# Moving sums, centring and small factors of the last stages from VectorE to GpSimd in a two-layer attention and expert kernel

## The reference

```python
x = x + attention(layernorm(x), ctx, mask)        # layer 0: softmax over the unmasked rows of ctx
x = x + experts(layernorm(x), Wr, Wg, Wu, Wd)     # 8 experts, the 2 best of each row, SiLU
x = x + topk_attention(layernorm(x), W_q, W_o, ctx)  # keeps the 54 largest of 1601 scores of each row
x = x + bitffn(layernorm(x), w1, w2)

def bitlinear(x, w):                              # used twice, with gelu between
    xs = 127.0 / clip(max(abs(x), axis=-1), 1e-5);  xq = clip(round(x * xs), -128, 127) / xs
    ws = 1.0 / clip(mean(abs(w)), 1e-5);            wq = clip(round(w * ws), -1, 1) / ws
    return einsum('bsd,hd->bsh', xq, wq)
```

## Time and profile before

| what | value |
|---|---|
| time, median of 3 runs (lowest, highest) | 443.55 us (442.79, 444.75) |
| profiled execution: its time, its span | 437.4 us, 435.7 us |
| busy of the span: PE, DVE, ACT, POOL | 81%, 69%, 42%, 11% |
| chain that ended last, by engine | PE 43%, DVE 31%, issue 13%, DMA 7% |

### The profile page before, as it was taken

One profiled execution on the slowest core, in us unless ns is written; L12 is line 12 of the kernel. 1 busy time (PEld: TensorE's weight loads), 2 busy tenths in 40 slices (PEclk: granted clock), 3 DMA queues, 4 the chain that ended last, 5 costly groups with the idle time before them and its releaser, 6 DMA issues.

```text
span 435.7 us, 6602 instructions
## 1 busy us (share of the span) xinstructions
PE 353.8 (81%) x2075; PEld 282.1 (65%) x2082; DVE 299.9 (69%) x760; ACT 181.5 (42%) x312; POOL 49.4 (11%) x100
## 2 busy tenths in 40 slices
PE   0899999999899996089898989878968872656984
PEld 0466777777799895047578988766655561625863
DVE  2432445762311024537999999999999999999983
ACT  2062353442534233024337255437656610443485
POOL 4100000115000001760000000170100000000010
PEclk9999999999999999559999999989998995969899
DMA  7583886609478992845878996453450031413301
GB/s 251 178 260 116 296 301 215 185 25 346 146 230 265 308 292 90 251 160 188 249 229 265 294 326 202 153 157 121 118 185 14 0 118 46 116 35 105 114 15 48
DMA packets 70809, 76.38 MB, mean 175 GB/s; under 512 B 5356, under 2 KB 69496, under 8 KB 70776
## 3 DMA queue, kind: packets, MB, share of 16 engines
q1 hardware_dynamic: 57272, 59.93, 44.0%
q10 hardware_dynamic: 11968, 11.84, 8.3%
q0 software_dynamic: 1536, 4.20, 2.9%
HBM read 66.91 MB, written 9.04 MB: 174 GB/s over the span
## 4 chain that ended last, share of the span: by engine, by line
PE 43%; DVE 31%; issue 13%; DMA 7%; ACT 2%; POOL 1%; SPq 1%; ACTq 0%; DVEq 0%; POOLq 0%
PE S L868 13%; PE GU L946 9%; DVE fold L1233 6%; DVE cand_h L1221 6%; PE A L895 6%; DVE cand_l L1228 5%; PE O L956 4%; DVE fold L1238 3%; PE A L899 3%; PE T L882 3%; DMA xg<-xs 2%; DMA v_sb<-ctx 2%; DVE row L1261 2%; DMA x_res<-x 2%; DVE gabs L1327 2%
## 5 line engine op out<-in xcount | busy, mean ns | idle before, releaser
L637 ACT ACTIVATE pT<-T 128x512 f32<-128x512 f32 x64 | 31.4, 514 | 79.0 <-PE T L882 74.9
L899 PE MATMUL A<-pT,v_sb 128*128 128x128 f32 (+1 forms) x416 | 54.1, 287 | 8.1 <-ACT pT L637 4.7
L946 PE MATMUL GU<-xgT,wg_ring 128*128 128x128 f32 x480 | 58.6, 276 | 2.1 <-DVE hid L1160 1.1
L946 PEld LDWEIGHTS GU<-xgT,wg_ring 128*128 128x128 f32 x480 | 56.9, 192 | 4.3 <-issue 1.9
L899 PEld LDWEIGHTS A<-pT,v_sb 128*128 128x128 f32 (+1 forms) x416 | 51.6, 202 | 10.9 <-issue 6.6
L1221 DVE MAX8 cand_h<-fold 128x8 f32<-128x801 f32 x56 | 55.0, 991 | 0.0
L868 PE MATMUL S<-k_sb,qT 128*128 128x400 f32 (+2 forms) x128 | 47.6, 518 | 4.4 <-ACT qT L694 1.3
L895 PE MATMUL A<-v_sb,pT 128*128 128x256 f32 (+1 forms) x208 | 49.6, 381 | 0.9 <-DMA v_sb<-ctx 0.9
L868 PE MATMUL S<-k_sb,xT 128*128 128x400 f32 (+2 forms) x128 | 48.5, 515 | 0.8 <-ACT xT L622 0.8
L1233 DVE MATCH_REPLACE8 fold<-cand_h,fold 128x801 f32<-128x801 f32 x48 | 47.1, 984 | 0.0
L895 PEld LDWEIGHTS A<-v_sb,pT 128*128 128x128 f32 (+1 forms) x208 | 37.9, 190 | 7.7 <-DMA v_sb<-ctx 1.5
(11 more groups left out here) (153 smaller groups left out, 488.4 us busy)
## 6 DMA issues: line engine op xcount, KB each, us to landing
v_sb<-ctx SPq DMA_DIRECT2D x36, 512.0 KB, 4.2
wg_ring<-Wg SPq DMA_DIRECT2D x30, 256.0 KB
wg_ring<-Wu SPq DMA_DIRECT2D x30, 256.0 KB
wd_ring<-Wd SPq DMA_DIRECT2D x30, 256.0 KB
k_sb<-ctxT SPq DMA_DIRECT2D x16, 400.0 KB, 5.4
xg<-xs ACTq DMA_DIRECT2D x30, 128.0 KB, 3.8
ys<-y_sb ACTq DMA_DIRECT2D x30, 128.0 KB, 3.5
k_sb<-ctxT SPq DMA_DIRECT2D x8, 402.0 KB, 4.2
```

The costliest lines, as they stand in the source:

```text
L637: act.activation(pT[0:r, i % NPT, :, :].rearrange("p a s -> p (a s)")[:, 0:w], t_bank("pT", *key)[0:r, 0:w], ACT.Copy).then_inc(pTe_done, 1)
L899: mm = pe.matmul(A_bank[:, o * P:(o + 1) * P], v[0:r, a, o * P:(o + 1) * P], pT[0:r, j, a, :], start=m == 0 and o == 0, stop=m == NMC - 1 ...
L946: mm = pe.matmul(gu_bank(*key)[:, a * F + f * P:a * F + (f + 1) * P], wg_ring[:, w % NWG, a, k, f * P:(f + 1) * P], cols[:, k, :], start=k ...
```

## The change

Seven steps move to other engines, for some or all tiles. For tiles 0 to 5 the sum `x3` becomes two steps: `x3a` (ACT takes the product out of PSUM, scaled, into `xn4`) and `x3p` (POOL adds it to `x_res`). `fin` becomes `fina` and `finp` in the same way; tiles 6 and 7 keep `x3` and `fin` on DVE. For all eight tiles `cent`, `va4`, `xmx`, `xscl`, `xdeq` and `gdeq` move from DVE to POOL. `cut`, the masking, stays on DVE. `WIDE_FROM` goes from 9 to 6, so the values of tiles 6 and 7 go round through five homes, three of which held layer 0's values. `ORDER` is written anew throughout; the second weight's `wqb` comes later in it.

```diff
+SUM_POOL = (0, 1, 2, 3, 4, 5)
-WIDE_FROM = 9
+WIDE_FROM = 6
...
 # gpsimd block
+                elif op == "x3p":
+                    t = key[0]
+                    pool.wait_ge(x3a_done, n("x3a", t))
+                    pool.wait_ge(norm_done, n("norm", 3, ROW_OF[t]))
+                    pool.tensor_tensor(x_res[:, t, :], xn4[:, t % 2, :], x_res[:, t, :], ALU.add).then_inc(x3p_done, 1)
+                elif op == "finp":
+                    t = key[0]
+                    pool.wait_ge(fina_done, n("fina", t))
+                    pool.tensor_tensor(fin[:, t % 2, :], fin[:, t % 2, :], x_res[:, t, :], ALU.add).then_inc(finp_done, 1)
...
+                elif op == "va4":
+                    pool.tensor_scalar(var4[:, t:t + 1], mv4[:, t, 1:2], EPS, None, ALU.add).then_inc(va4_done, 1)
...
+                elif op == "cent":
+                    pool.tensor_scalar(xn4[:, t % 2, :], x_res[:, t, :], mv4[:, t, 0:1], None, ALU.subtract) \
+                       .then_inc(cent_done, 1)
...
 # scalar block
+                elif op == "x3a":
+                    act.wait_ge(wo_done, n("wo", t))
+                    act.wait_ge(rc3_done, n("rc3", t))
+                    if t >= 2:
+                        act.wait_ge(q4_done, n("q4", t - 2))
+                    act.activation(xn4[:, t % 2, :], O_bank[:, 0:D], ACT.Copy, scale=r3[:, t:t + 1]).then_inc(x3a_done, 1)
+                elif op == "fina":
+                    act.wait_ge(dn_done, n("dn", t))
+                    act.wait_ge(gdeq_done, n("gdeq", t))
+                    act.activation(fin[:, t % 2, :], O_bank[:, 0:D], ACT.Copy, scale=gdeq[:, t:t + 1]).then_inc(fina_done, 1)
...
 # vector block: va4, cent, xmx, xscl, xdeq, gdeq are gone; st4 waits for x3p_done for tiles 0 to 5
-                elif op == "xscl":
-                    dve.scalar_tensor_tensor(out=xscl[:, t:t + 1], in0=xinv[:, t:t + 1], scalar=127.0,
-                                             in1=rstd4[:, t:t + 1], op0=ALU.mult, op1=ALU.mult).then_inc(xscl_done, 1)
...
 # ORDER, its end
-ginv.7 fin.5 gmul.7 gdeq.7 dn.6 store.5 h4T.7 fin.6
-h4e.7 store.6 dn.7 fin.7 store.7
+ginv.7 fin.6 gdeq.7 gmul.7 store.6 h4T.7 h4e.7 dn.7 fin.7 store.7
```

More of the change, by code:

```diff
@@ L137 @@
-merge.3 va4.1 thr.3 wo.2 upd.6.1 rs4.1 exp3.3 gabs.0.0 s3.4.1 xmx.1 stats.3.3 x3.2 gabs.0.1 st4.2 s3e.4.0 aggr.3.3
-gmx.0 s3e.4.1 ag4.2 s3.4.2 xinv.1 ginv.0 var.3.3 xdeq.1 gmul.0 gdeq.0 rstd.3.3 cut.3.0 s3.4.3 s3e.4.2 xscl.1 va4.2
-cent.2 xmul.1 rs4.2 s3.5.0 norm.3.3 s3e.4.3 xabs.2 xmx.2 pairH.4 s3.5.1 ldk.3.3.0 s3e.5.0 pairL.4 pT.3.3.0 maxH.4.0
-ldk.3.3.1 s3e.5.1 s3.5.2 pTe.3.3.0 maxL.4.0 h4T.0 repH.4.0 ldk.3.3.2 s3e.5.2 s3.5.3 h4e.0 xdeq.2 maxH.4.1 q4.1
-pvm.3.3.0 repL.4.0 ldk.3.3.3 s3e.5.3 q4e.1 repH.4.1 up.1.0 maxL.4.1 ldv.3.3.2 up.1.1 gelu.1.0 dn.0 xinv.2 maxH.4.2
@@ new lines @@
+cut.7.0 up.5.0 gelu.5.1 cut.7.1 pT.3.7.0 gelu.5.0 cut.7.2 pT.3.7.1 pTe.3.7.0 cut.7.3 rc3.7 pTe.3.7.1 pvm.3.7.0
+gabs.5.0 rc3.6 x3.6 st4.6 ag4.6 gabs.5.1 pT.3.7.2 cent.6 pvm.3.7.1 gmx.5 va4.6 pTe.3.7.2 xabs.6 rs4.6 ginv.5 gabs.4.1
+gmul.5 xmx.6 xdeq.6 xinv.6 gabs.4.0 xscl.6 pT.3.7.3 pvm.3.7.2 gdeq.5 xmul.6 gmx.4 pTe.3.7.3 ginv.4 gdeq.4 gmul.4 q4.6
+pvm.3.7.3 q4e.6 h4T.4 aTe.7 up.6.1 h4e.4 wo.7 gelu.6.1 up.6.0 x3.7 h4T.5 gelu.6.0 st4.7 dn.4 ag4.7 gabs.6.1 h4e.5
+cent.7 gabs.6.0 va4.7 fina.4 rs4.7 gmx.6 dn.5 ginv.6 xabs.7 gdeq.6 gmul.6 xmx.7 xdeq.7 xinv.7 xscl.7 finp.4 xmul.7
```

260 lines of the change are left out of this document (131 added, 129 removed).

## The result

The changed kernel took 449.68 us (median of 4 runs, 448.32 to 454.17), the kernel before in the same session 443.17 (4 runs, 442.35 to 444.75): slower by 6.5 us where 4.5 less were forecast, and outside the range of 433.5 to 445.0. Either way the changed kernel is slower; whether by more than 2% is open. Its profiled execution took 449.24 us with a span of 447.5. That of the kernel before, 437.4 us, was shorter than all its runs counted in the medians, so the 11.8 us between the two spans are more than the 6.5 between the medians.

A forecast was written before the change was run, and what follows sets the result against it. VectorE was taken to bound the second half, from first fold to last masking. Fold start 201.1, stretch 204.8 and tail 25.3 gave a 431.2 us span against 435.7, 4.5 less, so 439.0 us; range 433.5 to 445.0.

The forecast's parts named there:

- Term 2: Start of the fold: last down ends at 171.6, fold starts 29.5 us after it at 201.1, 2.4 us later than before.
- if the fold starts after 206: One sign, read from the changed profile's first fold, that would prove the prediction wrong; 201 (198 to 205) was expected.
- Term 1: VectorE's stretch from first fold to last masking: 41 instructions removed gain 7.3 us, new waits cost 0.5; 204.8 us.
- Term 3: Tail after the last masking: 25.3 us (24 to 27.5), against 25.4 before.
- the homes' gain: In the tail, five value homes let tile 7's products start earlier: up to 2.5 us, of which 1.0 was left.
- third rival: GpSimd and VectorE exclude each other on wide operands in the stretch: 11.2 us lost, 450.2 us; chance 0.08.
- second rival: At the group boundary PE idles 8 us and its clock falls; fold 6.5 us late, 443.1 us; chance 0.14.
- "Slower": Outcome for the whole kernel: a measured time above 445.8 us; chance 0.09.

The follow-up runs named there:

- rank_later: Changed kernel with the second group's ranking and expert 14's gate/up weights behind expert 10's down, downs 11 to 13 one product later; 452.42 us, ratio 1.025.
- scatters_held: rank_later with the second group's eight scatters made to wait for the first group's last gate and up product; ratio 1.028.
- crossed orders: Orders swapped at the fold's first step: old front with changed fold and engines, 459.27 us (1.039); changed front with old fold and engines, 453.55 us (1.032).
- order_alone: Changed kernel's order and five homes, with every sum, centring and small factor back on VectorE; 459.54 us, ratio 1.041 to the kernel before.
- moves_alone: Kernel before with its order and nine homes kept, only the engine moves of the change made; 445.88 us, ratio 1.013.
- beside_cut: Kernel before plus 28 GpSimd sums that nothing waits for, released beside maskings and replacements; one run, stretch 218.8 us against 211.6.
- neighbours_apart: Changed kernel with sixteen VectorE fold instructions moved up one to three places to part dependent neighbours; 451.80 us, ratio 1.022.

## Why the prediction was wrong

**Term 2 is the step that failed:** "The router, 1.06 us, and the rank move ahead of it, and three `down` stand in a row ...: I take 2.0 us, so the last `down` ends at 171.6. The rest of PE's first half has the same work." It ended at 182.9. The work is the same; what I priced was its duration on PE, and what it costs is what queues behind it: `down.0.10` behind `GU.0.12` and the transposes that wait for their rows, SyncE's queue behind `wd.0.13`, the last weights. That the places of these steps cost 3.6 us of the last product is shown (rank_later). I had named the shared `O_bank` as what each `down` waits for; the ranking gives it back at 164.8, 2.5 us before `down.0.10` starts.

The second part is transfers: I noted that "all eight scatters are now issued before", and took them only as a time after which a load may start, not as something that reaches the last products; holding them gave 3.8 us of the last `mul` (scatters_held, on top of rank_later). Both gone, from `mul.0.9` to the last `mul` it takes 19 us, 23 in the changed kernel, 15 behind the old front; those 4 us stay open. So do the 4.5 us by which `mul.0.9` itself was late, where I allowed a microsecond either way (between the middles of the eleven and eight profiles below it is 3.2).

From the last `down` to the fold 28.5 us were measured, 29.5 forecast: 17.1 of the 17 to tile 0's normalised rows, and 11.4 of the 12.5 from there. That match was partly luck: in scatters_held that distance is 36.1 us, since the scatters and the muls ahead hold the fold too. No run brought the last `down` forward and the fold with it, so that the fold follows from the last `down` is read from the trace, while that the front as a whole costs the 12.7 us is shown by the crossed orders. The condition "if the fold starts after 206" was the right one to watch.
Part of the 12.7 us is the two profiles' own scatter, but little: eight kernels with the old front whose fold no expert held start it at 198.7 to 202.0, eleven with the new one at 211.4 to 214.5; the middles, 200.5 and 213.1, are as far apart.

**Term 1.** The removal was sized well: 7.3 us forecast, 7.6 us of busy time between order_alone and the changed kernel, 6.0 between before and moves_alone. What I took as zero is what the new order does to VectorE's own work. I counted steps in and out (they cancel) and not their neighbours: order_alone is busy 213.4 us, 4.2 more than before. Its order has 23 adjacent pairs in which the second waits for the first (26 in the changed kernel's, none in the kernel before), at 0.11 us some 2.5 us of it; the other 1.7 stay open. So between the two kernels of the prediction VectorE's busy time fell by 3.5 us and not by 7.3, and of the waits, forecast 0.5, the rest grew by 1.5 us (2.4 to 3.9).

**Term 3.** Tile 7's products ran without a wait for values, and its `x3` started 9.4 us after the last masking, 10.0 before: 0.6 kept of the homes' gain, where I took 1.0. From there to the end 17.0 us, 15.4 before. Of these 1.6 us the chain from `x3` to `xmul`, through GpSimd, has 1.4 (4.4 us against 3.0) where I took 0.9, within its bounds, since centring takes 0.95 us and not 0.7, and `xmx` 0.30 or more. moves_alone has it too (27.7).

**The rule.** By the Trainium skill, SBUF — State Buffer, "Who interferes with whom", VectorE with two SBUF inputs and a reading GpSimd exclude each other; I held against it. The runs decide for the rule: 1.38 to 1.69 us for sums beside such an instruction against 0.73, 1.94 against 0.31 for a factor, and beside_cut. In the earlier trace rows the two start 0.01 us apart, and GpSimd's may have been first. Other traces have the same power further from a masking's start: started 0.19 us ahead of a masking it took 0.72 us and the masking 1.89, so neither loses (neighbours_apart, 321.13); started 0.17 us within one it took 2.28 (moves_alone, 312.79). So the earlier trace rows may show a power that came first, and says nothing of one that comes second. The third rival had the right mechanism at the wrong price: 14 of the 28 sums in beside_cut were aimed at a masking, and in its one run the stretch grew by 7.2 us, of which VectorE's busy time is 1.9 and the rest waits. In the changed kernel its visible waits for GpSimd are the 0.62 and 0.62 us ahead of `st4` and 0.72 ahead of `xinv.1`, some 2 us, not 11.2. The Trainium skill, GPSIMD Engine Reference, 3.1, gives 1.96 times VectorE's time for a sum of 2048 columns; here, with 256, 0.73 us against 0.48 is 1.5 times, and centring, 0.95 against 0.35, 2.7.

**Rivals and chances.** The measured case, a boundary that costs more than the engines give, was my second rival in kind, priced at 443.1 with the clock as its reason. The clock was not it: from tile 0's rows to the fold it took 11.4 us, less than the 12.5 forecast. "Slower" had 0.09, and that was the real error: every cost at the boundary was bounded by the durations of the steps moved, so the bounds shared one blind spot.
